# Window values in the full attention's buffer, the top-k choice as a mask on the exponentials, and a new order of work

## The reference

```python
def _self_attn(h, ...):                       # windows of 128 tokens, shifted by 64
    qkv = jnp.roll(h @ w_qkv + b_qkv, -SHIFT, axis=1).reshape(B, nw, WIN, 3, H, D)
    attn = softmax(einsum('bnqhd,bnkhd->bnhqk', q, k) / sqrt(D))
    o = einsum('bnhqk,bnkhd->bnqhd', attn, v)
def _topk_cross_attn(h, ctx, ...):
    scores = einsum('bqhd,bkhd->bhqk', q, k) / sqrt(D)
    top_s, top_i = jax.lax.top_k(scores, 16)  # 16 of 77 context tokens for each query and head
    attn = softmax(top_s)
    o = einsum('bhqk,bhqkd->bqhd', attn, take_along_axis(v, top_i))
def _swiglu(h, ...):
    u = h @ w_m1 + b_m1                       # 2048 wide, in the other layers 1024
    return silu(u[..., :1024]) * u[..., 1024:] @ w_m2 + b_m2
```

## Time and profile before

| | |
|---|---|
| median of 3 runs | 2931.4 us (2920.38 to 2933.68) |
| profiled execution | 2928.1 us |
| its span | 2925.9 us, 47617 instructions |
| TensorE busy | 2736.6 us, 94% |
| VectorE busy | 1884.0 us, 64% |
| ScalarE busy | 1415.4 us, 48% |
| GpSimd busy | 711.6 us, 24% |

### The profile page before, as it was taken

One profiled execution on the slowest core, in us unless ns is written; L12 is line 12 of the kernel. 1 busy time (PEld: TensorE's weight loads), 2 busy tenths in 40 slices (PEclk: granted clock), 3 DMA queues, 4 the chain that ended last, 5 costly groups with the idle time before them and its releaser, 6 DMA issues.

```text
span 2925.9 us, 47617 instructions
## 1 busy us (share of the span) xinstructions
PE 2736.6 (94%) x15077; PEld 1352.8 (46%) x15133; DVE 1884.0 (64%) x4177; ACT 1415.4 (48%) x2575; POOL 711.6 (24%) x1063
## 2 busy tenths in 40 slices
PE   8999999999989998999988898899899998999899
PEld 5344344335535324334455566666554423224456
DVE  6977387643565874866354688668966784885620
ACT  4454635574455683566644343323123584775431
POOL 2100001131331111231134455443411010112420
PEclk9999999999999999999999999999999999999899
DMA  6233023323542312332166526421501322113621
GB/s 212 59 110 116 29 71 100 102 77 92 169 147 53 116 49 72 94 109 70 50 194 181 147 83 191 126 83 61 164 23 33 101 63 56 45 53 111 182 89 38
DMA packets 268152, 286.78 MB, mean 98 GB/s; under 512 B 70665, under 2 KB 207243, under 8 KB 267275
## 3 DMA queue, kind: packets, MB, share of 16 engines
q1 hardware_dynamic: 256651, 282.28, 32.8%
q0 software_dynamic: 11264, 1.46, 0.3%
HBM read 167.43 MB, written 114.72 MB: 96 GB/s over the span
## 4 chain that ended last, share of the span: by engine, by line
PE 69%; DVE 12%; issue 7%; DMA 6%; POOL 3%; SPq 2%; ACT 1%; DVEq 0%; ACTq 0%; POOLq 0%
PE ring_c L1457 12%; PE ring_b L1424 12%; PE ring_a L1380 10%; PE ring_b L1480 7%; PE ring_a L1492 7%; PE ring_b L1423 3%; PE ring_a L1469 3%; PE ring_b L1337 3%; DVE row_max L1743 2%; PE ring_a L1480 2%; DMA q_ring<-neg_max_parts 2%; PE ring_b L1451 1%; PE ring_b L1412 1%; DVE topk_marks L1768 1%; DVE topk_marks L1762 1%
## 5 line engine op out<-in xcount | busy, mean ns | idle before, releaser
L1565 ACT ACTIVATE probs<-ring_b 128x512 f32<-128x512 f32 (+1 forms) x1728 | 918.0, 600 | 414.1 <-PE ring_b L1424 352.2
L1743 DVE TENSOR_REDUCE row_max<-ring_a 128x1 f32<-128x1024 f32 x512 | 601.8, 1216 | 156.3 <-PE ring_a L1380 154.8
L1424 PE MATMUL ring_b<-q_ring,k_ring 100*128 100x512 bf16 x1536 | 525.5, 380 | 15.6 <-ACT probs L1565 2.8
L1380 PE MATMUL ring_a<-k_ring,q_ring 96*128 96x512 bf16 x1536 | 448.3, 382 | 30.5 <-DVE row_max L1743 15.9
L1457 PE MATMUL ring_c<-probs,v_and_ones 128*17 128x512 f32 x3072 | 403.0, 600 | 1.5 <-ACT probs L1565 0.9
L1856 POOL CAST neg_max_parts<-neg_max 16x128 bf16<-16x128 f32 x112 | 34.8, 310 | 1329.6 <-ACT neg_max L1559 1133.5
L1740 DVE CUSTOM_DVE_ANT_0 w_mlp<-ring_a,w_mlp 128x1024 bf16<-128x1024 f32 x256 | 302.0, 1221 | 62.6 <-PE ring_a L1380 61.8
L1424 PEld LDWEIGHTS ring_b<-q_ring,k_ring 100*128 100x128 bf16 x1536 | 145.0, 97 | 346.3 <-issue 236.1
L1380 PEld LDWEIGHTS ring_a<-k_ring,q_ring 96*128 96x128 bf16 x1536 | 134.7, 98 | 256.5 <-issue 159.8
L1480 PE MATMUL ring_b<-h_feat,w_mlp 128*128 128x512 f32 x512 | 233.1, 601 | 9.5 <-issue 9.0
L1787 DVE TENSOR_TENSOR x_tok<-x_tok,ring_a 128x512 f32<-128x512 f32 x96 | 65.5, 684 | 255.9 <-PE ring_a L1492 161.8
(11 more groups left out here) (144 smaller groups left out, 3503.9 us busy)
## 6 DMA issues: line engine op xcount, KB each, us to landing
q_ring<-scr_q SPq DMA_DIRECT2D x128, 384.0 KB, 4.3
scr_q<-split SPq DMA_DIRECT2D x64, 384.0 KB, 2.9
k_ring<-scr_k SPq DMA_DIRECT2D x64, 384.0 KB, 5.4
scr_q<-split SPq DMA_DIRECT2D x64, 256.0 KB, 3.1
scr_out<-out_stage SPq DMA_DIRECT2D x128, 128.0 KB, 2.4
scr_out<-out_stage SPq DMA_DIRECT2D x64, 256.0 KB, 3.0
h_feat<-scr_out SPq DMA_DIRECT2D x56, 256.0 KB
reciprocals<-scr_recip SPq DMA_DIRECT2D x56, 256.0 KB
```

The costliest lines, as they stand in the source:

```text
L1380: last = mm(ps[:, half * BLOCK:(half + 1) * BLOCK], q[0:PARTS, h, t * P:(t + 1) * P], k_view(g)[0:PARTS, h, half * BLOCK:(half + 1) * BLOC ...
L1424: last = mm(ps[:, :], k_view(g)[0:ROWS, h, s.kt * P:(s.kt + 1) * P], q[0:ROWS, h, q0:q0 + BLOCK], start=not g.masked, stop=True)
L1565: f(PT[0:n, s.pt, :], ps[0:n, :], ACT.Exp, **kw).then_inc(b_evac, 1)
L1743: v.tensor_reduce(NM[:, s.nm, s.u:s.u + 1], ps, AX.X, ALU.max).then_inc(a_evac, 1)
```

## The change

Three edits; of the new tables the diff shows one row. First, L2 keeps its values in `VA` as the other layers do; the pool `VW` goes, with the ones written each time, the masks' waits and the wait of `w1`. Second, the top-k choice: `tk_mark` is cut into `tk_half` (first 8) and `tk_mark` (next 8). GpSimd only subtracts the largest score (`tk_shift`), after the first half. ScalarE takes the exponential of all 77 scores while VectorE marks the next 8. Then one VectorE operation (`tk_mask`) makes 1 of a mark and 0 of the rest and multiplies it into the exponentials; the transposes and the next step's first write to `topk_marks` wait for that. Third, the tables of ranks are new, and with them the order of all five lists.

```diff
-    mod=(-12, -12, -12, -9),
+    mod=(4.1, -7, -12, -8),
...
@@ def values
-        st.vplace = "VW" if st.akind == "window" else "VA"
-        _, last, _ = yield ("get", st.vplace)
+        _, last, _ = yield ("get", "VA")
@@ def weights
-        if name == "w1" and LAYERS[l]["kind"] == "window":
-            _, s, _ = yield ("get", "VW")
-            if s is not None:
-                rel.append(s)
@@ def topk_units, topk_rest
-                s = yield do("tk_mark", [("DVE", 5.95)], after=[k, s3_last], counts=["tk_n"], of=k, s3=s3, s3_last=s3_last)
-                p.spawn(topk_rest(st, key, g, unit, k, s), rank_of("tk_s", st.l, st.b, st.blks[0]))
+                half = yield do("tk_half", [("DVE", 2.95)], after=[k, s3_last], counts=["half_n"], of=k, s3=s3, s3_last=s3_last)
+                p.spawn(topk_rest(st, key, g, unit, k, half), rank_of("tk_s", st.l, st.b, st.blks[0]))
+                s = yield do("tk_mark", [("DVE", 2.95)], after=[half], counts=["tk_n"], of=k, half=half)
+                p.raise_flag(key + ("marked", g.n, hp), s)
-        s = yield do("tk_args", [("POOL", 5.23)], after=[mark], counts=["tkarg_n"], of=k, mark=mark)
-        p.give("S3", mark.s3, s)
+        s = yield do("tk_shift", [("POOL", 1.37)], after=[half], counts=["tkarg_n"], of=k, half=half)
         e = yield do("tk_exp", [("ACT", 0.605)], after=[s], counts=["tkexp_n"], of=k, arg=s, fn="exp")
+        mark = yield ("flag", key + ("marked", g.n, k.hp))
+        e = yield do("tk_mask", [("DVE", 0.75)], after=[e, mark], counts=["tkmask_n"], of=k, e=e, mark=mark)
+        p.give("S3", half.s3, e)
@@ tensor
-                    pe.wait_ge(tk_exp, s.e.tkexp_n + 1)
+                    pe.wait_ge(tk_masked, s.e.tkmask_n + 1)
@@ vector
+                elif s.kind == "tk_mask":
+                    k = s.of
+                    dve.wait_ge(tk_sel, s.mark.tk_n + 1)
+                    dve.wait_ge(tk_exp, s.e.tkexp_n + 1)
+                    v.scalar_tensor_tensor(out=TS[:, k.ts], in0=S3[:], scalar=GONE * 0.9, in1=TS[:, k.ts], op0=ALU.is_le, op1=ALU.mult)\
+                        .then_inc(tk_masked, 1)
@@ gpsimd
-                elif s.kind == "tk_args":
+                elif s.kind == "tk_shift":
                     k = s.of
-                    pool.wait_ge(tk_sel, s.mark.tk_n + 1)
-                    link(g_.tensor_scalar(S3[:], S3[:], GONE * 0.9, -1.0e30, ALU.is_gt, ALU.mult))
+                    pool.wait_ge(tk_half, s.half.half_n + 1)
                     m = M8[:, k.ts, :, 0:1].broadcast_to([P, 8, CTX])
-                    link(g_.tensor_tensor(out=TS[:, k.ts], in0=TS[:, k.ts], in1=m, op=ALU.subtract))
-                    g_.tensor_tensor(out=TS[:, k.ts], in0=TS[:, k.ts], in1=S3[:], op=ALU.add).then_inc(tk_arg, 1)
+                    g_.tensor_tensor(out=TS[:, k.ts], in0=TS[:, k.ts], in1=m, op=ALU.subtract).then_inc(tk_arg, 1)
```

More of the change, by code:

```diff
@@ L570, in values @@
         row = None
-        st.vplace = "VW" if st.akind == "window" else "VA"
-        _, last, _ = yield ("get", st.vplace)
+        _, last, _ = yield ("get", "VA")
         p.raise_flag(key + ("vplace",), None)
-        masks = []
-        if st.vplace == "VW" and last is None:
-            for f in ("mask_read", "mask_done"):
-                s = yield ("flag", f)
-                masks.append(s)
         if LAYERS[l]["vbias"][0]:
@@ L582, in values @@
             h = yield ("flag", key + ("h", BLOCKS - 1 if st.akind == "window" else blk))
-            s = yield do("v", [("PE", 3.453), ("DVE", 1.33)], after=[h, w, last, row] + masks, ring="a", l=l, b=b, u=blk, last=last, row=row,
-                         h=h, w=w, masks=masks)
+            s = yield do("v", [("PE", 3.453), ("DVE", 1.33)], after=[h, w, last, row], ring="a", l=l, b=b, u=blk, last=last, row=row,
+                         h=h, w=w)
         if row is not None:
@@ L801, in mlp @@
             p.give("W1", 0, Step(rel=list(fl.w1_users[l].values())))
-            if cfg["kind"] == "window":
-                p.give("VW", 0, s)
         x = []
@@ L1015, in bcast @@
             return ap.unsqueeze(1).broadcast_to([ap.shape[0], n, ap.shape[-1]])
-        def v_tile(l):
-            return VW if LAYERS[l]["kind"] == "window" else VA
         def w1_view(l):
@@ L1706, in _ @@
                                 dve.wait_ge(pv_done, s.last.pv_n + 1)
-                        elif LAYERS[s.l]["kind"] == "window":
-                            dve.wait_ge(a_evac, s.masks[0].an + 1)
-                            dve.wait_ge(b_full, s.masks[1].bn + 1)
-                        if LAYERS[s.l]["kind"] == "window":
-                            v.memset(place[:, s.u * 4:s.u * 4 + 4, :, HEAD:VU], 1.0)
                     else:
@@ L1759, in _ @@
                     if s.s3_last is not None:
-                        dve.wait_ge(tk_arg, s.s3_last.tkarg_n + 1)
+                        dve.wait_ge(tk_masked, s.s3_last.tkmask_n + 1)
                     for i in range(8):
                         last = v.match_replace(S3[:, i, :], M8[:, k.ts, i, :], TS[:, k.ts, i, :], GONE)
-                    link(last)
+                    last.then_inc(tk_half, 1)
+                elif s.kind == "tk_mark":
+                    dve.wait_ge(tk_half, s.half.half_n + 1)
                     for i in range(8):
```

64 lines of the change are left out of this document (30 added, 34 removed).

## The result

The changed kernel is slower: ratio 1.0039, 95% interval 1.0026 to 1.0052. That is 11 us more, where 15 less were forecast. The medians of 13 runs each, 2940.05 and 2924.69 us, lie 15 us apart; they mix all runs, among them one of the changed kernel at 3898 us under a granted clock of 0.65, which the ratio leaves out. A second comparison (after_again) gave 1.0036 (1.0024 to 1.0047). The time lies inside the range, the sign is wrong.

What follows compares the result with a forecast made beforehand. Third-layer slack on TensorE was 191 us, with VectorE the limit late and VectorE-GpSimd waits earlier. Terms -7-2-4-6+4+0 = -15 us gave 2913 us from 2928.1; forecast's own range 2902 to 2922, full range 2885 to 2946.

Steps and rivals of the forecast that it cites:

- The order elsewhere: All layers: new order moves nearly nothing outside L2; taken as 0, with 10 us either way.
- (a): L2, 1640 to 1760 us: VectorE's 11.4 us of waits for GpSimd go, masks take 4.3 back; 7 us gained.
- (b): L2, 2000 to 2125 us: VectorE operations stretched beside GpSimd shorten; 9 us gained, 2 net of eight masks.
- The mask's price: New VectorE mask in L2's top-k: 0.85 us each, 32 in all; eight in the VectorE-bound stretch cost 6.8 us.
- The bound of 1.9 us: L2's top-k: upper bound for one mask on VectorE if stretched beside GpSimd, instead of 0.85 us.
- The mask's wait: L2's top-k, VectorE: mask waits for the exponential only if ScalarE is busy; costed at nothing.
- The chain to the transposes: L2, last mark to transposes: 0.85 us instead of 5.2 plus 0.7; 4 us gained, bounds 0 and 14.
- The up weights: Before L2's first MLP product: W1's load no longer waits for the window's last product; 6 us gained, bounds 0 and 10.
- The values: L2's first window values must wait for the second layer's last product; 4 us lost, bounds 0 and 10.
- Rival 1: In-order TensorE: waits removed at one place come up at the next; 2930 us, chance 0.20.
- Rival 2: L2's top-k: late exponential makes the mask hold up VectorE's queue; 2913 + 20 w, 2953 at w = 2 us; chance 0.18.
- 41 more fillers: Whole order: fillers rise from 1757 to 1798, 5 us if each stands for a real wait; costed at 0.

Runs made afterwards that it cites:

- after_again: The changed kernel run once more against the kernel before, nothing else changed: ratio 1.0036.
- both_old_order: Kernel before, its order held, with shared place of values and top-k part; exponential from 4.6 us, mask from 6.2 us behind the marks' planned start: 1.0030.
- room of 8.0: Kernel before, order held, top-k part added, exponential from 8.0 us, mask from 9.5 us behind the marks' planned start: 0.9950; with shared place of values too, 0.9973.
- new_choice_old_order: Kernel before, its order held, with the top-k part alone; exponential from 4.6 us, mask from 6.2 us behind the marks' planned start: 1.0027.
- place_mended: Changed kernel with two entries moved near 1490 us, loads ahead of writes on SyncE, row maxima ahead of a normalisation on VectorE: 1.0056 to the kernel before.
- four re-planned versions: Kernel before, planner ordering anew, with only the new table (1.017), both parts under old table (1.0107), top-k alone (1.0057) or shared values alone (1.0071).

## Why the prediction was wrong, step by step

**The step that failed is "The order elsewhere": "I take 0, with 10 us either way".** With the order held and room for the mask, both parts of the change give 850.2 us for steps 2196 to 2900 where before took 864.7 (mean of two). The changed kernel takes 875.4 (mean of two). So its order costs 25 us against the held one in these profiles, and by the ratios of the whole kernel (1.0039 and 0.9973) 19 us: about twice the bound that I had set. What an order costs depends on what it is held against: with the smaller room (both_old_order, 871.8 us, ratio 1.0030) the held order is nearly as slow as the new one. So the parts can win, but only in an order that gives them room, and the new one does not.

That the held order gives -14.5 us where the sum had -15 is in part luck. 7.7 of the 14.5 are time between steps (197.6, mean of two, to 189.9); the other 6.8 are in the steps themselves (667.2 to 660.3), for which the sum has no term. The whole kernel won only 8 us (0.9973). And the fillers and idle time before the first MLP product hardly moved in the held order, 10.1 and 10.7 to 8.8 us, where the sum had 6. Time between steps in five pieces shows where the new order loses:

| steps | before (two) | both parts, held order | changed (two) |
|---|---|---|---|
| 2196 to 2309 | 13.6, 16.7 | 15.4 | 24.1, 23.1 |
| 2310 to 2499 | 59.6, 58.9 | 59.8 | 54.4, 55.5 |
| 2500 to 2649 | 43.3, 44.4 | 41.4 | 56.9, 57.7 |
| 2650 to 2739 | 66.0, 67.7 | 61.1 | 61.1, 59.4 |
| 2740 to 2900 | 12.0, 12.9 | 12.1 | 11.4, 11.4 |

The same number is not quite the same work in two orders, so these are stretches rather than steps. Against before, 8 us were lost at the first window attention and 13 in the middle (about 1780 to 2000 us; 16 against the held order), 4 were won between the two, and the late stretches won 8. The middle has no single wait. In steps 2500 to 2649 TensorE's time before transposes of chosen scores rose from 1.5 and 1.0 to 8.4 and 9.0 us, and before output projections from 0.0 to 8.4 us; before MLP products into `ring_b` it fell from 10.1 and 10.7 to 4.9 us. More than half of it is fillers, put where the planner saw TensorE wait. In the changed kernel:

```profile
1858.08 3.66 PE L1277 MATMUL ring_b<-ident_f 128*128 128x256 bf16 x32
1863.15 1.10 PE L1420 MATMUL ring_b<-ident_f,topk_scores 128*77 128x128 f32 x8 [1.41 <-DVE topk_scores L1757]
...
1866.26 2.90 PE L1277 MATMUL ring_a<-ident_f 128*128 128x256 bf16 x25
1872.10 3.27 PE L1458 MATMUL ring_a<-w_out,h_feat 128*128 128x256 f32 x8 [2.95 <-DVE h_feat L1769]
```

Why the planner's table gives this order is not something that these runs can say, and a single mended entry did not give the time back.

By the other steps:
- (a), the wait for GpSimd: gone entirely, 16.3 us over the layer. The mechanism was right; masks' waits of 7.6 us and the masks' own time stand against it.
- (b), the stretching: L1681 and L1682 back at 692 and 426 ns (forecast near 0.7 and 0.55), L1675 only to 921. Right, for two of three: not all subtractions came while VectorE searched maxima, two met L1675. The prediction's "In (a) and (b) the rule and the trace agree" fits (b) alone; (a) is a wait, and shows nothing of shared interfaces.
- The mask's price: 793 ns against 0.85, right. The bound of 1.9 us was too low. With the room of 8.0 the median was again 793 ns, but the longest took 2.67 us, beside a GpSimd operation of 2.35 us. First GpSimd, then VectorE:

```profile
1935.09 2.35 POOL L1871 TENSOR_TENSOR x_tok<-x_tok,gate 128x1024 f32<-128x1024 f32 x1 [3.13 <-DVE x_norm L1666]
...
1935.43 2.67 DVE L1792 SCALAR_TENSOR_TENSOR topk_scores<-topk_marks,topk_scores 128x616 f32<-128x616 f32 x1
```

  It began 0.34 us after GpSimd and ended 0.66 us after it: it hardly moved until GpSimd was done. It is not always VectorE that is held up. In new_choice_old_order a mask began 0.26 us ahead of the same kind of GpSimd operation, kept its 793 ns, and GpSimd took 2.75 us. GpSimd, then VectorE:

```profile
1748.39 2.75 POOL L1871 TENSOR_TENSOR x_tok<-x_tok,gate 128x1024 f32<-128x1024 f32 x1 [2.13 <-DVE x_norm L1666]
...
1748.13 0.79 DVE L1792 SCALAR_TENSOR_TENSOR topk_scores<-topk_marks,topk_scores 128x616 f32<-128x616 f32 x1
```

  In the changed kernel no mask met a GpSimd operation of this size (784 to 800 ns). The Trainium skill names the condition, VectorE with two SBUF inputs (GPSIMD Engine Reference, Key points), and the trace agrees.
- The mask's wait: 7.6 us in two waits in the changed kernel, little. I had asked after VectorE alone. ScalarE stands in order too, and waited 62.7 us for GpSimd before the exponentials from 1475 to 2125 us (27.1 in the held order with room of 8.0). It had waited 90.5 us there before, so the sum of these waits does not tell the loss; what stands behind each does.
- The chain to the transposes, -4: not won in the changed kernel (14.1 to 13.6 us of idle time), won with room (5.2 us). A mechanism that the order must make use of.
- The up weights, -6: right ahead of the product 10.24 us of fillers and idle time became 5.24, -5. The size was right, by luck: the load stood in SyncE's queue until 1905.00, long after the window's last product, and took 11.0 us to land (9.4 before), and TensorE was idle for 2.92 and 0.73 us just ahead of these fillers.
- The values, +4: fillers around the place 23, 1.69 + 0.50 + 0.82 = 3.0 us. That size was right, and in the held order (0.9993) the shared place is harmless. The idle 5.95 and 4.38 us behind it were not in the sum.
- Rival 1, "the waits only move" (2930), was nearest for the whole, and place_mended shows it at work. Rival 2's mechanism is real but belongs to new_choice_old_order, not to the changed kernel. I gave too little to the sign that was in the order itself: 41 more fillers, which I had costed at nothing.

Left open: which of the new order's choices costs the middle stretch its 13 to 16 us; what made the clock of the steps differ; and whether the held order gains more with the top-k part alone (0.9950) than with both (0.9973). Steps 2196 to 2900 say no, 849.8 and 850.2; the difference lies before step 2196 (1422.5 and 1431.6 us), where the two programs run the same queues.

## What to carry to other kernels

When a change brings a new order with it, forecast the operations and the order as two terms, and price the order from what its waits and fillers say, with a bound as wide as other orders lie apart (here the four re-planned versions were 17 to 50 us slower than before). To find what the operations are worth, hold the order and edit its queues by hand, with more than one room: here a loss of 0.4% became a gain of 0.3% (both parts) or 0.5% (the top-k part alone), and with too little room it stayed a loss of 0.3%. An operation that becomes ready early must not be queued early as well: ask of every in-order engine what stands behind it while it waits.

## What the runs showed of the hardware

- A VectorE operation with two SBUF inputs took up to 2.67 us instead of 0.79 when it began 0.34 us behind a GpSimd operation on 128x1024, three times its price. I had expected twice. When it began 0.26 us ahead of one, it kept its 0.79 us and GpSimd took 2.75 us, where its median is 2.36.
- A wait of TensorE can cost a second time in the matmuls behind it: behind 5.95 us of idle time 16 window products took 1.87 us at a granted clock of 0.62, and the next 16 took 1.06 us. Whole steps differ as well: with the same matmuls, those of 2196 to 2900 took 653 to 668 us in versions of one order.
- The same queues up to step 2196 gave 1422 to 1434 us in versions of one order: that much of a difference between two profiles need not be an effect of an edit further on.
